# Turned probabilities copied by ScalarE alone, and a second PSUM tile for the first head's relative scores, in a relative-position cross attention

## The chip, the cores and the metric

One core of a Trainium2 chip runs the whole program. The metric is the device time of one execution in microseconds, taken as the median of the runs shown. All times below count from the start of the profiled span.

## What is computed

The program is a chain of six layers, each added to x. The change lies in the fourth, the cross attention of the second block (`cross1`):

```python
content = einsum('bthd,bThd->bhtT', q + r_w_bias, k)
rel = einsum('bthd,bThd->bhtT', q + r_r_bias, pe)   # pe: projected sinusoids
rel = _relative_shift(rel)
attn = (content + rel) * (1.0 / sqrt(HEAD_DIM))
attn = attn * mask - 10000000000.0 * (1.0 - mask)
p = softmax(attn, axis=-1)
out = einsum('bhtT,bThd->bthd', p, v).reshape(b, t, DMODEL)
```

There are 256 query tokens, 4096 keys, 16 heads of 16 columns, all in float32. The shift moves every row of the relative scores by an amount that depends on the row, across the whole matrix.

## The kernel before, in words

**Units.** The scores of one head are 256 x 4096. They are cut into four units (`U` = 4): two tiles of 128 query rows by two halves of 2048 keys. A unit has two parts of 1024 keys (`SUB`), and the layer has 64 units (`UNITS`).

**The way of a unit.** TensorE makes the relative scores of a part in the PSUM tile `rel_ps` (`relative`, L1821; four matmuls in all use two 32-row groups of the array, part 0 the first two groups and part 1 the last two). ScalarE copies them to `out0` or `out1` (`evacuate`, L1928). SP stores the unit's 1 MB to DRAM (`store`, L1774) with a row pitch one longer than the row, and reads it back shifted, a part at a time, into `row` (`read_back`, L1763). TensorE makes the content scores in `cont_ps` (`content`, L1821), VectorE adds them to `row` (`add`, L2011), GpSimd multiplies by the mask (L1989), VectorE adds the mask's complement `minus` and takes the maximum (`top_of`, L2020), ScalarE takes the exponential (L1933). Then TensorE turns a part by eight 128x128 transposes into `turn_ps` (`turn`, L1852), it is copied to `turned`, and TensorE weighs the values with it (`weigh`, L1867). The sums go through `sumsT` (VectorE, L2041) and one more matmul (`bring_together`, L1876) to `o_all` (L2046).

**Who copies what is turned.** Part 0 is copied by ScalarE whole (L1939, 1024 columns). Part 1 is copied half by ScalarE (`copy_left`, L1946, 512 columns) and half by VectorE (`copy_turned`, L2035, 512 columns).

**The order.** It is written out by hand. Every engine runs `slots`: slot n works on the relative scores of unit n+4, the content scores, sum and mask of unit n, the maximum and exponential of unit n-1, the turning and weighing of unit n-2, and the gathering of unit n-3. Slots -4 to 2 and the last ones are written out, and the others stand in a hardware loop over pairs of heads. Slots -4 to -1 therefore hold only the first head's relative scores and the second head's queries (`turn_weights` L1969, the product L1840, `make_queries` L2072). I call them the opening. In them TensorE and ScalarE take turns on the one tile `rel_ps`. VectorE makes `minus` (L2082) ahead of all slots. In TensorE's program the second part of unit n+3 comes first in slot n, ahead of the content scores of unit n.

## Time and profile before

| | |
|---|---|
| median of 3 runs | 1489.84 us (1487.76 to 1493.67) |
| profiled execution, its own time | 1488.5 us |
| its span | 1486.7 us |
| busy shares of the span | TensorE 80%, VectorE 65%, ScalarE 60%, GpSimd 26% |
| this layer | from about 736 us to 1307 us for the part with the slots |

A row of the timeline gives the start, the duration, the engine and the line; PE is TensorE's matmul, PEld its weight load, DVE is VectorE, ACT ScalarE, POOL GpSimd, SPq SP's DMA queue. The brackets hold the idle time of the engine before the instruction and what released it. `xN` means N instructions merged into a row. L1821 is one line for both kinds of scores, so the tile's name tells them apart.

### The profile page before, as it was taken

What the parts mean: (1) busy time and instruction counts of PE and PEld (TensorE: products, weight loads), DVE (VectorE), ACT (ScalarE), POOL (GpSimd) and SP (SyncE); (2) the same over time, 40 slices, a digit from 0 to 9 for tenths busy, and PEclk for the clock granted to TensorE, in tenths of its full rate; (3) what the DMA queues carried; (4) which work ended last, traced back from release to release, by engine and by line L of the source; (5) the groups of instructions that cost most, each with busy time, mean ns of one, the idle gap of its engine ahead of it and who ended that gap; (6) DMA issues with size and microseconds to landing.
All of it is one profiled execution on the core that took longest, in us unless ns stands there. A gap on an engine that the chain in (4) does not pass through costs nothing. (4 is left out here: it accounts for less than half of the span.)

```text
span 1486.7 us, 25581 instructions
## 1 busy us (share of the span) xinstructions
PE 1195.8 (80%) x8423; PEld 716.1 (48%) x8423; DVE 969.3 (65%) x1633; ACT 894.2 (60%) x1243; POOL 383.8 (26%) x149
## 2 busy tenths in 40 slices
PE   7677777739999768799768888888888888746798
PEld 3343344324444446688624544444444444424587
DVE  5798898950110566522228999999999999835321
ACT  3699999948889335233226666676766667413210
POOL 1000000000000040000006767676676766600000
PEclk9899999969999778899957999999999999877899
DMA  7864544448552420044648888888888888251050
GB/s 264 269 169 111 120 121 106 100 102 158 109 105 45 163 89 1 29 145 152 219 159 300 283 286 275 285 283 285 290 278 286 274 289 282 96 162 59 1 170 7
DMA packets 97048, 257.51 MB, mean 173 GB/s; under 512 B 11193, under 2 KB 41305, under 8 KB 85466
## 3 DMA queue, kind: packets, MB, share of 16 engines
q1 hardware_dynamic: 96992, 256.79, 55.7%
q8 instruction: 32, 0.52, 0.1%
q14 instruction: 24, 0.20, 0.0%
HBM read 165.31 MB, written 91.92 MB: 173 GB/s over the span
## 5 line engine op out<-in xcount | busy, mean ns | idle before, releaser
L1989 POOL TENSOR_TENSOR xb_row<-xb_row,w_mask 128x1024 f32<-128x1024 f32 x128 | 359.3, 2827 | 376.0 <-DVE xb_row L2011 376.0
L2020 DVE CUSTOM_DVE_ANT_0 xb_row<-xb_row,xb_minus 128x1024 f32<-128x1024 f32 x128 | 266.6, 2083 | 8.4 <-POOL xb_row L1989 8.2
L1928 ACT COPY xb_out<-xb_rel_ps 128x1024 f32<-128x1024 f32 x128 | 129.9, 1015 | 132.3 <-PE xb_rel_ps L1821 132.1
L2011 DVE TENSOR_TENSOR xb_row<-xb_cont_ps,xb_row 128x1024 f32<-128x1024 f32 x128 | 155.2, 1213 | 24.7 <-PE xb_cont_ps L1821 24.2
L1852 PEld LDWEIGHTS xb_turn_ps<-_ident,xb_row 128*128 128x128 f32 x1024 | 118.5, 149 | 103.5 <-ACT xb_row L1933 52.0
L1821 PE MATMUL xb_rel_ps<-xb_kk,xb_qq 32*128 32x512 f32 x512 | 157.3, 692 | 10.8 <-ACT xb_out L1928 9.5
L567 DVE TENSOR_REDUCE xa_stats<-xa_b_ps 128x1 f32<-128x1024 f32 x128 | 153.2, 1220 | 7.3 <-PE xa_b_ps L466 7.1
L828 ACT ACTIVATE xa_probs<-xa_psT,xa_t_now 128x1024 f32<-128x1024 f32 x128 | 141.2, 1114 | 25.3 <-PE xa_psT L787 25.2
L1821 PE MATMUL xb_cont_ps<-xb_kk,xb_qq 32*128 32x512 f32 x512 | 152.6, 673 | 2.9 <-DVE xb_row L2011 2.9
L1852 PE MATMUL xb_turn_ps<-_ident,xb_row 128*128 128x128 f32 x1024 | 151.2, 295 | 4.3 <-ACT xb_row L1933 2.3
L516 ACT ACTIVATE xa_exps<-xa_b_ps,xa_stats 128x1024 f32<-128x1024 f32 x128 | 142.7, 1115 | 3.6 <-DVE xa_stats L567 2.1
L1484 POOL TENSOR_TENSOR b_tc<-b_raw,w_waves 128x512 f32<-128x512 f32 x4 | 5.1, 1269 | 533.4 <-ACT b_raw L1470 533.4
L1933 ACT ACTIVATE xb_row<-xb_row,xb_ntop 128x2048 f32<-128x2048 f32 x64 | 128.3, 2005 | 0.0
L1867 PE MATMUL xb_sum_ps<-xb_turned,xb_vhead 128*17 128x128 f32 x2048 | 86.5, 296 | 24.8 <-DVE xb_turned L2035 24.8
L466 PE MATMUL xa_b_ps<-xa_k,xa_q 96*128 96x512 bf16 x256 | 77.5, 388 | 25.7 <-ACT xa_exps L516 13.8
L575 DVE CUSTOM_DVE_ANT_0 xa_squares<-xa_exps 128x1024 f32<-128x1024 f32 x64 | 78.4, 1225 | 25.1 <-ACT xa_exps L516 25.1
L487 PE MATMUL xa_b_ps<-xa_wv,xa_ctxT 128*128 x512 | 67.0, 285 | 17.9 <-ACT xa_exps L516 17.9
L760 PE MATMUL xa_sums<-xa_probs,xa_vhead 128*17 128x256 f32 x1024 | 80.8, 389 | 0.2 <-ACT xa_probs L828 0.2
L1655 DVE SCALAR_TENSOR_TENSOR _x<-b_out_ps,b_gates,_x 128x256 f32<-128x256 f32 x64 | 27.9, 479 | 78.6 <-PE b_out_ps L1570 78.1
L487 PEld LDWEIGHTS xa_b_ps<-xa_wv,xa_ctxT 128*128 128x128 f32 x512 | 61.3, 196 | 33.2 <-ACT xa_exps L516 29.3
L1867 PEld LDWEIGHTS xb_sum_ps<-xb_turned,xb_vhead 128*17 128x17 f32 x2048 | 48.0, 102 | 57.3 <-DVE xb_turned L2035 42.8
L1946 ACT COPY xb_turned<-xb_turn_ps 128x512 f32<-128x512 f32 x64 | 37.5, 586 | 60.2 <-PE xb_turn_ps L1852 60.0
(364 smaller groups left out, 1868.3 us busy)
## 6 DMA issues: line engine op xcount, KB each, us to landing
xb_row<-rel_scores SPq DMA_DIRECT2D x128, 512.0 KB, 5.3
rel_scores<-xb_out SPq DMA_DIRECT2D x32, 1024.5 KB, 4.9
rel_scores<-xb_out SPq DMA_DIRECT2D x32, 1024.0 KB, 4.8
b_e_w<-in_L_ffn_e_w SPq DMA_DIRECT2D x32, 513.0 KB, 3.4
w_w<-in_L_ffn_w SPq DMA_DIRECT2D x24, 512.0 KB, 6.8
xa_k<-first_parts SPq DMA_DIRECT2D x24, 384.0 KB, 5.1
value_rows<-xa_values SPq DMA_DIRECT2D x16, 544.0 KB, 6.1
xb_kk<-key_blocks SPq DMA_DIRECT2D x17, 512.0 KB, 6.3
```

The source lines that it names most:

```text
L487: mm = nc.tensor.matmul(out[:, n * P:(n + 1) * P], ctxT[:, k, at:at + P], wv[:, bass.ds(it, 1), k, :], start=(k == 0), stop=(k == KC - 1))
L516: nc.scalar.activation(exps[:, u % 4], ps[:, slot % 4], ACT.Exp, scale=-1.0, bias=stats[:, c % 2, 0, u:u + 1], accum_out=stats[:, c % 2, 1 ...
L567: nc.vector.tensor_reduce(stats[:, c % 2, 0, u:u + 1], ps[:, slot % 4], AX, ALU.min).then_inc(s["min_ready"], 1)
L828: nc.scalar.activation(probs[:, g % 4].rearrange("p c n -> p (c n)"), ps[:, g % 2], ACT.Exp, scale=t_now[:, b:b + 1]).then_inc(probs_ready, 1)
L1821: mm = nc.tensor.matmul(out[:, k * BANK:(k + 1) * BANK], qq[rows, b, kind, t * P:(t + 1) * P], kk[rows, b, half], start=True, stop=True)
L1852: mm = nc.tensor.transpose(turn_ps[:, k * P:(k + 1) * P], row[:, u, at:at + P], f.ident[:])
L1867: mm = nc.tensor.matmul(sum_ps[at:at + DV, 0:P], vhead[:, b, half * NCH // 2 + part * CPS + k, :], turned[:, part, k, :], start=(part == 0 ...
L1928: nc.scalar.copy(out[:, part * SUB:(part + 1) * SUB], rel_ps[:]).then_inc(s["rel_out"], 1)
L1933: nc.scalar.activation(row[:, u], row[:, u], ACT.Exp, bias=ntop[:, u:u + 1]).then_inc(s["exp_done"], 1)
L1989: nc.gpsimd.tensor_tensor(row[:, u, at:at + SUB], row[:, u, at:at + SUB], mask[:, t, half * HALF + at:half * HALF + at + SUB], ALU.mult).t ...
L2011: nc.vector.tensor_tensor(row[:, u, at:at + SUB], cont_ps[:], row[:, u, at:at + SUB], ALU.add).then_inc(s["cont_out"], 1)
L2020: nc.vector.tensor_tensor_reduce(out=row[:, u, at:at + SUB], in0=row[:, u, at:at + SUB], in1=minus[:, t, half * HALF + at:half * HALF + at ...
```

## The change

1. ScalarE copies both parts of what is turned, 1024 columns each. VectorE's copy and the semaphore `turned_left` are gone.
2. In slots -4 to -1 TensorE makes both parts of a unit's relative scores: part 0 in `rel_ps` as before, part 1 in `cont_ps`, which is unused until slot 0 (`first_right`). ScalarE copies part 0 (and counts two on `rel_out`), VectorE copies part 1 (`evacuate_right`, with the new semaphore `fill_out`). The store of a first-head unit waits for both, and the first content scores wait for VectorE's last copy. The second part of unit 3, which stood first in slot 0, is now in slot -1.
3. VectorE makes the two tiles of `minus` in slots -2 and -1, each behind its copy, instead of ahead of all slots. The first `top_of` waits for both.

```diff
 def store(p, c):
     sp.wait_ge(s["rel_out"], 2 * n + 3)
+    if isinstance(n, int) and n < U:
+        sp.wait_ge(s["fill_out"], n + 1)
...
 def content(p, c, part):
     pe.wait_ge(s["cont_out"], 2 * n + part + 1)
+    if part == 0 and isinstance(n, int) and n == 0:
+        pe.wait_ge(s["fill_out"], U)
...
+def first_right(c):
+    if c > 0:
+        pe.wait_ge(s["fill_out"], c)
+    scores(0, c, 1, 1, cont_ps, s["rel_mm"])
...
 # TensorE's slot
-if runs(n, U - 1):
+if runs(n, U - 1) and (n is None or n > 0):
     relative(p, c + U - 1, 1)
...
 if runs(n, U):
     relative(p, c + U, 0)
+if n is not None and n < 0:
+    first_right(c + U)
...
 # ScalarE
-nc.scalar.copy(out[:, part * SUB:(part + 1) * SUB], rel_ps[:]).then_inc(s["rel_out"], 1)
+first = isinstance(n, int) and n < U
+nc.scalar.copy(out[:, part * SUB:(part + 1) * SUB], rel_ps[:]).then_inc(s["rel_out"], 2 if first else 1)
...
-nc.scalar.copy(turned[:, 1, 0:CPS // 2].rearrange("p k n -> p (k n)"), turn_ps[:, 0:BANK]
-               ).then_inc(turned_left, 1)
+act.wait_ge(s["turned"], 2 * n + part + 1)
+act.wait_ge(s["weighed"], 2 * n + part + 1)
+nc.scalar.copy(turned[:, part].rearrange("p k n -> p (k n)"), turn_ps[:]).then_inc(turned_sb[part], 1)
...
 # VectorE
+def evacuate_right(c):
+    dve.wait_ge(s["rel_mm"], 2 * c + 2)
+    if c >= NHALF:
+        dve.wait_ge(rel_stored[c - NHALF], 16)
+    out = out1 if c % NHALF else out0[:, 1:HALF + 1]
+    nc.vector.tensor_copy(out[:, SUB:HALF], cont_ps[:]).then_inc(s["fill_out"], 1)
...
-nc.vector.tensor_copy(turned[:, 1, CPS // 2:].rearrange("p k n -> p (k n)"), turn_ps[:, BANK:]
-                      ).then_inc(turned_sb[1], 1)
...
 # VectorE's slot, and the lines ahead of the slots
+if n is not None and n < 0:
+    evacuate_right(c + U)
+if n is not None and -NT <= n < 0:
+    t = n + NT
+    nc.vector.tensor_scalar(minus[:, t], mask[:, t], 1.0, 1e10, ALU.subtract, ALU.mult
+                            ).then_inc(s["minus_set"], 1)
...
-for t in range(NT):
-    nc.vector.tensor_scalar(minus[:, t], mask[:, t], 1.0, 1e10, ALU.subtract, ALU.mult
-                            ).then_inc(s["minus_set"], 1)
-dve.wait_ge(s["minus_set"], NT)
```

TensorE's queue in the opening before (`xb_both` with `xb_wturn` is the product that makes queries):

```order
L1840 MATMUL xb_both<-xb_xnT,xb_wturn 128x256 x2
L1821 MATMUL xb_rel_ps<-xb_kk,xb_qq 128x512 x4
L1840 MATMUL xb_both<-xb_xnT,xb_wturn 128x256 x2
L1821 MATMUL xb_rel_ps<-xb_kk,xb_qq 128x512 x12
L1821 MATMUL xb_cont_ps<-xb_kk,xb_qq 128x512 x2
L1821 MATMUL xb_rel_ps<-xb_kk,xb_qq 128x512 x2
L1821 MATMUL xb_cont_ps<-xb_kk,xb_qq 128x512 x2
```

And the same place with the change:

```order
L1850 MATMUL xb_both<-xb_xnT,xb_wturn 128x256 x2
L1822 MATMUL xb_rel_ps<-xb_kk,xb_qq 128x512 x2
L1822 MATMUL xb_cont_ps<-xb_kk,xb_qq 128x512 x2
L1850 MATMUL xb_both<-xb_xnT,xb_wturn 128x256 x2
L1822 MATMUL xb_rel_ps<-xb_kk,xb_qq 128x512 x2
L1822 MATMUL xb_cont_ps<-xb_kk,xb_qq 128x512 x2
L1822 MATMUL xb_rel_ps<-xb_kk,xb_qq 128x512 x2
L1822 MATMUL xb_cont_ps<-xb_kk,xb_qq 128x512 x2
L1822 MATMUL xb_rel_ps<-xb_kk,xb_qq 128x512 x2
L1822 MATMUL xb_cont_ps<-xb_kk,xb_qq 128x512 x4
L1822 MATMUL xb_rel_ps<-xb_kk,xb_qq 128x512 x2
L1822 MATMUL xb_cont_ps<-xb_kk,xb_qq 128x512 x2
```

The query products keep their places. Every unit's two parts stand as a pair in two tiles, and the first content scores (the last two of the row with x4) follow the fourth pair directly.

VectorE's queue in the opening before:

```order
L2079 TENSOR_TENSOR xb_qbias<-xb_qbias,xb_rbias 128x17
L2072 TENSOR_SCALAR xb_qq<-xb_both,xb_qbias,xb_kinds 128x256 x2
L2082 TENSOR_SCALAR xb_minus<-w_mask 128x4096 x2
L2072 TENSOR_SCALAR xb_qq<-xb_both,xb_qbias,xb_kinds 128x256 x2
L2011 TENSOR_TENSOR xb_row<-xb_cont_ps,xb_row 128x1024 x2
```

And with the change:

```order
L2087 TENSOR_TENSOR xb_qbias<-xb_qbias,xb_rbias 128x17
L2080 TENSOR_SCALAR xb_qq<-xb_both,xb_qbias,xb_kinds 128x256 x2
L2012 COPY xb_out<-xb_cont_ps 128x1024 x2
L2080 TENSOR_SCALAR xb_qq<-xb_both,xb_qbias,xb_kinds 128x256 x2
L2012 COPY xb_out<-xb_cont_ps 128x1024
L2058 TENSOR_SCALAR xb_minus<-w_mask 128x4096
L2012 COPY xb_out<-xb_cont_ps 128x1024
L2058 TENSOR_SCALAR xb_minus<-w_mask 128x4096
L2020 TENSOR_TENSOR xb_row<-xb_cont_ps,xb_row 128x1024 x2
```

Four copies are new, and the two tiles of `minus` stand behind the third and the fourth.

## Rows read from the trace of the kernel before

**Rows 1.** Windows view, steady part. Engines' busy us (instructions), TensorE clock, DMA share, GB/s
```profile
1000.00:1050.00 50.00, 41.94 (x424) 24.22 (x428) 48.12 (x73) 34.60 (x33) 34.99 (x14) 0.97 0.84 286
```

**Rows 2.** Timeline, GpSimd: start us, duration us, engine, line, operation, [idle before <-releaser]
```profile
777.14 2.34 POOL L1989 TENSOR_TENSOR xb_row<-xb_row,w_mask 128x1024 f32<-128x1024 f32 x1 [217.69 <-DVE xb_row L2011]
780.62 3.26 POOL L1989 TENSOR_TENSOR xb_row<-xb_row,w_mask 128x1024 f32<-128x1024 f32 x1 [1.13 <-DVE xb_row L2011]
...
802.25 5.61 POOL L1989 TENSOR_TENSOR xb_row<-xb_row,w_mask 128x1024 f32<-128x1024 f32 x2 [2.50 <-DVE xb_row L2011]
...
1005.12 5.61 POOL L1989 TENSOR_TENSOR xb_row<-xb_row,w_mask 128x1024 f32<-128x1024 f32 x2 [2.50 <-DVE xb_row L2011]
...
1289.10 5.60 POOL L1989 TENSOR_TENSOR xb_row<-xb_row,w_mask 128x1024 f32<-128x1024 f32 x2 [2.50 <-DVE xb_row L2011]
```

**Rows 3.** Timeline, VectorE, one pass of the loop
```profile
1004.97 1.21 DVE L2020 CUSTOM_DVE_ANT_0 xb_row<-xb_row,xb_minus 128x1024 f32<-128x1024 f32 x1
...
1006.47 1.22 DVE L2011 TENSOR_TENSOR xb_row<-xb_cont_ps,xb_row 128x1024 f32<-128x1024 f32 x1
...
1007.61 0.68 DVE L2035 COPY xb_turned<-xb_turn_ps 128x512 f32<-128x512 f32 x1
...
1008.60 3.21 DVE L2020 CUSTOM_DVE_ANT_0 xb_row<-xb_row,xb_minus 128x1024 f32<-128x1024 f32 x1 [0.23 <-POOL xb_row L1989]
```

**Rows 4.** Timeline, TensorE and ScalarE, the same pass
```profile
1003.97 0.40 PE L1876 MATMUL xb_both<-xb_gather,xb_sumsT 128*128 128x17 f32 x2 [0.99 <-DVE xb_sumsT L2041]
...
1007.28 0.59 ACT L1946 COPY xb_turned<-xb_turn_ps 128x512 f32<-128x512 f32 x1 [0.80 <-PE xb_turn_ps L1852]
...
1008.34 0.63 PE L1867 MATMUL xb_sum_ps<-xb_turned,xb_vhead 128*17 128x128 f32 x16 [0.53 <-DVE xb_turned L2035]
...
1009.97 0.86 PEld L1852 LDWEIGHTS xb_turn_ps<-_ident,xb_row 128*128 128x128 f32 x8 [0.76 <-ACT xb_row L1933]
```

**Rows 5.** Timeline, the opening: first head's relative scores to the first add
```profile
748.63 4.48 DVE L2082 TENSOR_SCALAR xb_minus<-w_mask 128x4096 f32<-128x4096 f32 x2
...
751.03 1.01 ACT L1928 COPY xb_out<-xb_rel_ps 128x1024 f32<-128x1024 f32 x1 [5.56 <-PE xb_rel_ps L1821]
...
752.10 2.08 PE L1821 MATMUL xb_rel_ps<-xb_kk,xb_qq 32*128 32x512 f32 x4 [1.10 <-ACT xb_out L1928]
...
755.59 2.08 PE L1840 MATMUL xb_both<-xb_xnT,xb_wturn 128*128 128x256 f32 x4 [1.42 <-ACT xb_wturn L1969]
...
773.54 1.22 PE L1821 MATMUL xb_rel_ps<-xb_kk,xb_qq 32*128 32x512 f32 x2 [1.11 <-ACT xb_out L1928]
...
773.65 1.22 PE L1821 MATMUL xb_cont_ps<-xb_kk,xb_qq 32*128 32x512 f32 x2
...
775.84 1.23 DVE L2011 TENSOR_TENSOR xb_row<-xb_cont_ps,xb_row 128x1024 f32<-128x1024 f32 x1 [17.05 <-PE xb_cont_ps L1821]
```

**Rows 6.** DMA view, 736 to 800 us: transfers, KB each, median us to landing
```profile
xb_row<-rel_scores SPq DMA_DIRECT2D x9, 512.0 KB, 6.0
rel_scores<-xb_out SPq DMA_DIRECT2D x3, 1024.5 KB, 5.2
```

**Rows 7.** Timeline, SP's queue, the first read back
```profile
768.28 0.35 SPq L1763 DMA_DIRECT2D xb_row<-rel_scores  x1
```

**Rows 8.** Windows view, the opening's clock and DMA share (columns as in rows 1)
```profile
780.00:784.00 4.00, 3.26 (x9) 1.43 (x10) 2.89 (x4) 1.32 (x2) 3.26 (x1) 0.50 0.99 333
...
792.00:796.00 4.00, 4.00 (x17) 2.17 (x18) 3.03 (x7) 1.84 (x3) 2.37 (x1) 0.51 0.70 236
796.00:800.00 4.00, 3.56 (x52) 2.15 (x52) 3.92 (x3) 3.76 (x4) 3.27 (x2) 1.00 0.76 225
```

**Rows 9.** Timeline, the end of the loop
```profile
1299.17 0.59 ACT L1946 COPY xb_turned<-xb_turn_ps 128x512 f32<-128x512 f32 x1 [2.12 <-PE xb_turn_ps L1852]
...
1305.10 0.69 DVE L2035 COPY xb_turned<-xb_turn_ps 128x512 f32<-128x512 f32 x1 [3.77 <-PE xb_turn_ps L1852]
...
1305.85 0.63 PE L1867 MATMUL xb_sum_ps<-xb_turned,xb_vhead 128*17 128x128 f32 x16 [0.22 <-DVE xb_turned L2035]
```

More of the change, by code:

```diff
@@ L1847, in turn @@
                     pe.wait_ge(turned_sb[1 - part], n + 1)
-                    if part == 0:
-                        pe.wait_ge(turned_left, n + 1)
                     for k in range(CPS):
@@ L1858, in weigh @@
                     pe.wait_ge(turned_sb[part], n + 1 + part)
-                    if part == 1:
-                        pe.wait_ge(turned_left, n + 2)
                     if u == 0 and part == 0:
@@ L1933, in exponentials, with copy_turned @@
                     nc.scalar.activation(row[:, u], row[:, u], ACT.Exp, bias=ntop[:, u:u + 1]).then_inc(s["exp_done"], 1)
[L1935 removed]
+                def copy_turned(p, c, part):
                     n, head, u, b, t, half = where(p, c)
[L1937 to L1947 removed]
+                    act.wait_ge(s["turned"], 2 * n + part + 1)
+                    act.wait_ge(s["weighed"], 2 * n + part + 1)
+                    nc.scalar.copy(turned[:, part].rearrange("p k n -> p (k n)"), turn_ps[:]).then_inc(turned_sb[part], 1)
                 def slot(p, c, n):
                     if runs(n, -2):
[L1951 removed]
+                        copy_turned(p, c - 2, 0)
                     if runs(n, U):
@@ L1954, in slot @@
                     if runs(n, -2):
-                        copy_left(p, c - 2)
+                        copy_turned(p, c - 2, 1)
                     if runs(n, -1):
                         exponentials(p, c - 1)
-                    if runs(n, U):
+                    if runs(n, U) and (n is None or n >= 0):
                         evacuate(p, c + U, 1)
@@ L2017, in top_of @@
                     dve.wait_ge(s["masked"], 2 * n + part + 1)
+                    if part == 0 and isinstance(n, int) and n == 0:
+                        dve.wait_ge(s["minus_set"], NT)
                     dve.sem_inc(s["top_begun"], 1)
@@ L2029, in top_of @@
                                                 top2[:, u, 1:2], -1.0, ALU.max, ALU.mult).then_inc(s["top_kept"], 1)
-                def copy_turned(p, c):
-                    n, head, u, b, t, half = where(p, c)
-                    dve.wait_ge(s["turned"], 2 * n + 2)
-                    dve.wait_ge(s["weighed"], 2 * n + 2)
-                    nc.vector.tensor_copy(turned[:, 1, CPS // 2:].rearrange("p k n -> p (k n)"), turn_ps[:, BANK:]
-                                          ).then_inc(turned_sb[1], 1)
                 def sums_out(p, c):
@@ L2059, in slot @@
                         add(p, c, 1)
-                    if runs(n, -2):
-                        copy_turned(p, c - 2)
                     if runs(n, -3):
```

13 lines of the change are left out of this document (1 added, 12 removed).

## The prediction

> **What bounds the kernel now.** I read the windows view of the loop first. VectorE looks like the bound there: busy 48.12 of 50 us, ScalarE only 34.60 [rows 1]. That reading would make its copy the thing to remove. The timeline of GpSimd says otherwise. Its masks come in pairs of 5.61 us, each pair after an idle 2.50 us that VectorE's add ends [rows 2], and from 802.25 to 1289.10 us 60 slots pass in 486.85 us, 8.11 each, which is 5.61 + 2.50. The add that ends the idle time comes behind VectorE's 3.21 us maximum, and that row is stretched: the same instruction takes 1.21 at 1004.97 [rows 3]. The long one starts at 1008.60, just after the first mask of the pair that began at 1005.12, and ends at 1011.81, which is 1.08 after GpSimd's pair ends at 1010.73 [rows 2, 3]. So VectorE counts as busy while it waits for GpSimd's second mask. The loop is a ring: two masks, the last 1.08 of a maximum, a small copy, an add, and again the masks. The first mask of a pair is stretched too: 2.34 alone (777.14), 3.26 beside a maximum (780.62) [rows 2]; 5.61 is 2.34 + 3.27.
>
> The Trainium skill (SBUF — State Buffer, Who interferes with whom) says that GpSimd and VectorE share a port pair that one of them holds for a whole instruction, and that a VectorE instruction with two SBUF inputs meets a GpSimd one there. The trace agrees: 3.21 against 1.21. The same section lists copies among what can take the pair, under conditions on their operands; by that alone each of VectorE's 0.68 us copies would hold the masks up, and the change would give back some 60 x 0.68 = 41 us.
>
> Then the opening, 749 to 776 us. One tile is filled in 2.08 us and emptied in 1.01, in turn, so a part takes about 3.19 (751.03 to the end of the next matmuls at 754.18) [rows 5]. VectorE waits 17.05 us for the first content scores, and TensorE is what it waits for [rows 5].
>
> **Part 1, the copies in the loop.** Removed from VectorE: 0.68 us a slot [rows 3]. In the ring this buys nothing. VectorE's copy ends at 1008.29, and its next maximum cannot end before GpSimd's pair ends plus 1.08, whenever it starts. Without the copy VectorE waits 0.6 us longer for the same mask. I take 0; the ends are 0 and -0.68 a slot. Nor did the copy slow the masks: 3.27 in the loop with it, 3.26 at 780.62 without it [rows 2].
> Added to ScalarE: 1.01 instead of 0.59, +0.43 a slot (a 1024-column copy as at 751.03) [rows 4, 5]. ScalarE has some 15 us of 50 free [rows 1]. Three things wait behind that copy:
> - The weighing of part 1. It began at 1008.34, 0.05 after VectorE's copy. ScalarE's long copy, from 1007.28, ends at 1008.29 [rows 4]: no change.
> - The exponential, and behind it TensorE's transposes at 1009.97, which waited for it [rows 4]. They move to 1010.4 and end at about 1011.5. TensorE's next instruction waits for VectorE and comes one period after 1003.97, at 1012.08 [rows 4]. The slack was 1.0 and 0.6 is left.
> - ScalarE's next copies, in front of which it idles anyway.
> So 0 a slot. If 0.43 came through in every slot it would be +26.
>
> **Part 2, the opening.** Worked with 2.08 for the matmuls of a part, 1.01 for ScalarE's copy, 2.08 for the query product, 2.28 for one tile of `minus` (half of 4.48 and an overlap) [rows 5]. The new VectorE copy of 1024 columns from PSUM is not in the loop; the nearest rows are its add over the same PSUM columns, 1.23, and its 512-column copy, 0.68, which doubled gives 1.36 [rows 3, 5]. I take 1.22. Two parts in two tiles use different row groups. The trace shows such a pair at 773.54 and 773.65, side by side [rows 5], so a pair costs about 2.2 and not 4.2.
> - Unit 0: matmuls 748.9 to 751.1, copies out by 752.4.
> - ScalarE prepares the query weights (0.4) after one copy instead of two. The product runs 752.4 to 754.4; it was at 755.59 [rows 5].
> - Unit 1: 754.4 to 756.6, out by 757.9. Unit 2: 757.6 to 760.1, out by 761.4; then `minus` to 763.7. Unit 3: from 760.8, second part 761.5 to 763.5; VectorE is free at 763.7 and copies to 764.9; second `minus` to 767.1.
> - First content scores 764.9 to 767.0, first add at 767.3 instead of 775.84 [rows 5]: -8.5.
> - Another 0.9 follows. Before, unit 4's relative scores had to wait until unit 3's last part (773.54) was made and copied, to 776.7. Now they follow the content scores at 767.0, 9.7 earlier. Through ScalarE's copies they gate the next query product, hence the fourth add. From there everything runs 9.4 earlier.
> `minus` costs nothing: VectorE had 17 us to wait. It delays the last copy by 0.2.
> Do the transfers follow? The first read back was issued at 768.28 [rows 7], as the store of unit 1 landed. That store can now go at 758.0, and with 4.2 to 5.2 for landing [rows 6] the read back goes at 762.2 to 763.2, 5 to 6 us earlier. A read back takes 6.0 in the median [rows 6], so it lands by 768.2, near the 767.3 wanted. Between there and 784 the DMA engines were nearly full before (0.99) [rows 8], and VectorE never waited for them. I put them just outside the path.
> Sum for the opening: -9.4, with -5.5 as the small end (all shifts as the first read back does) and -12 as the large (TensorE at full clock one slot sooner).
>
> **Part 3, the end.** After the last masks nothing hides ScalarE's copy. Behind it stand two exponentials (the last starts after the copy at 1299.17) and the last weighing, which waited for VectorE's 0.69 us copy (1305.10, then 1305.85) [rows 9]. 0.43 + 0.43 + 0.32 = +1.2.
>
> **Sum.** -9.4 + 0 + 1.2 = -8.2. Against the profiled execution's 1488.5 us that gives 1480.3. The median of the runs is 1.3 higher and would give 1481.6. I say **1481**.
>
> **The rivals.**
> - **The transfers hold the opening.** For: the full DMA engines, and a read back that starts only 5 to 6 us earlier. Against: VectorE waited for TensorE, not for them. Opening -5.5, end +1.2: **1484.5**.
> - **The pairs do not overlap**, or the two copies hold each other up. A unit then takes some 5.3 instead of 6.4, four units give 4.4 in place of 8.5: also about 1485. Against: the pair at 773.54.
> - **The clock.** TensorE's granted clock was 0.50 from the opening until about 796 us, and rose after a stretch in which TensorE was busy without a gap (4.00 of 4.00) [rows 8]. If a denser opening lifts it one slot sooner, or the end runs at the full clock, 3 us more go: **1478**. The other way costs as much. The Trainium skill (TensorE: Matmul & The Clock Gate, Part 1) says that activity releases the half clock and that the same kernel shows different numbers of slow matmuls from run to run; by that this case is open in either direction.
> - **VectorE is the bound after all**, and the copy's 0.68 comes back 60 times: **1440**. Against: the 3.21 us rows.
> - **Slower: ScalarE's longer copy joins the ring.** It delays the exponential, the transposes behind it, and with them the content scores that VectorE adds. It decides once the transposes come over 1.0 us late; I count 0.43. In a slot with a query product, ScalarE's weight copy adds 0.4 to that, which leaves little, and at half clock the transposes take 1.0 longer. If 0.43 came through everywhere: 1480.3 + 26 = **1506**; in one slot in four, 1487.
>
> **How the numbers follow.** A measurement of this kernel tells about 0.5%, 7.4 us, from no change, so faster means below 1482.4. Forecast 0.60, its own range 1478.5 to 1483.5, of which 0.46 lies below 1482.4. Transfers 0.20, no overlap 0.03, both within 0.5%. Clock 0.07 and VectorE 0.04, both faster. ScalarE 0.06: slower 0.04, the mild form within 0.5% 0.02. Together faster 0.57, same 0.39, slower 0.04. The range of 1476 to 1487 takes in the forecast, the transfers, the clock and the mild form. The first read backs and the clock are its width.
>
> **What would show it.** Right: GpSimd's first mask near 768.5 instead of 777.14; the eight first-head copies in four pairs about 3.4 us apart; mask pairs still every 8.11 us, and VectorE idle for some 0.8 us ahead of the long maximum where it was 0.23; the loop reaching its pace near 793; the last mask pair near 1279.7; the stretch from there to the layer's last sums about 1.2 longer. Wrong: a period other than 8.11 (VectorE or ScalarE was in the ring), an add of the first three units released by a DMA, or pairs of matmuls in the opening that take over 4 us.

## The result, and the profile after

| | before | changed |
|---|---|---|
| median, 9 executions each on one chip | 1493.6 us (1487.76 to 1500.84) | 1485.21 us (1480.63 to 1491.19) |
| profiled execution, own time | 1488.5 us | 1491.19 us |
| its span | 1486.7 us | 1489.4 us |
| VectorE busy | 969.3 us | 941.3 us |
| ScalarE busy | 894.2 us | 913.0 us |
| GpSimd busy | 383.8 us | 386.6 us |

The ratio is 0.9954, with a 95% interval of 0.9935 to 0.9972: 6.8 us less, give or take 2.7 (the two medians differ by 8.4). The predicted 1481 was worked against a median of 1489.84 of three runs; on nine runs the same kernel came out at 1493.6, and 8.2 less than that is 1485.4.

The profiled execution of the change is the slowest of its nine, and its span is 2.7 us longer than the one before. So the two traces are not read by their spans but by landmarks inside the layer. All landmarks below count from the layer's first VectorE instruction (it clears the tile of the weighted sums, `xb_sum_ps`), which no part of the change touches: it started at 736.43 us before and at 741.52 in the changed trace, and those 5.1 us belong to earlier layers.

| from the layer's start, us | before | changed | moved by |
|---|---|---|---|
| GpSimd's first mask | 40.71 | 31.98 | -8.7 |
| unit 3's first mask | 65.82 | 54.96 | -10.9 |
| one slot, unit 3 to unit 60 | 8.11 | 8.11 | 0.0 |
| unit 60's first mask | 528.34 | 517.29 | -11.1 |
| last sums of the layer | 570.90 | 566.11 | -4.8 |
| from there to the end of the span | 179.35 | 181.78 | +2.4 |

The opening gave 10.9 us, the loop nothing, and the stretch from unit 60 to the layer's last sums took 6.3 back. Four views show how. The 2.4 us more behind the layer lie in a part of the program that the change doesn't touch; the account of the sum comes back to them.

**The loop.** Windows view of the changed kernel, columns as in [rows 1]:

```profile
1000.00:1050.00 50.00, 42.65 (x418) 24.26 (x418) 46.28 (x69) 36.29 (x33) 34.97 (x13) 0.97 0.86 290
```

VectorE is 1.84 us less busy in 50, ScalarE 1.69 more, and GpSimd stands at 34.97 as before. The timeline of one pass, changed kernel, to be held against [rows 2 to 4]:

```profile
999.26 5.61 POOL L1990 TENSOR_TENSOR xb_row<-xb_row,w_mask 128x1024 f32<-128x1024 f32 x2 [2.51 <-DVE xb_row L2020]
...
1001.42 1.01 ACT L1948 COPY xb_turned<-xb_turn_ps 128x1024 f32<-128x1024 f32 x1 [0.81 <-PE xb_turn_ps L1860]
...
1002.49 0.63 PE L1873 MATMUL xb_sum_ps<-xb_turned,xb_vhead 128*17 128x128 f32 x16 [0.54 <-ACT xb_turned L1948]
1002.73 3.22 DVE L2031 CUSTOM_DVE_ANT_0 xb_row<-xb_row,xb_minus 128x1024 f32<-128x1024 f32 x1 [0.82 <-POOL xb_row L1990]
```

The pair of masks is 5.61 again and the idle time ahead of it 2.51. The maximum still takes 3.22. VectorE waits 0.82 ahead of it where it waited 0.23: the time of the removed copy has become a wait for the same mask.

**The opening.** Timeline of the changed kernel, to be held against [rows 5] and [rows 7]:

```profile
756.28 1.23 DVE L2012 COPY xb_out<-xb_cont_ps 128x1024 f32<-128x1024 f32 x1 [2.38 <-PE xb_cont_ps L1822]
...
761.83 1.22 DVE L2012 COPY xb_out<-xb_cont_ps 128x1024 f32<-128x1024 f32 x1 [4.32 <-PE xb_cont_ps L1822]
...
765.23 1.23 DVE L2012 COPY xb_out<-xb_cont_ps 128x1024 f32<-128x1024 f32 x1 [1.27 <-PE xb_cont_ps L1822]
...
766.37 2.28 DVE L2058 TENSOR_SCALAR xb_minus<-w_mask 128x4096 f32<-128x4096 f32 x1
...
767.08 0.34 SPq L1762 DMA_DIRECT2D xb_row<-rel_scores  x1
...
768.29 1.01 ACT L1937 COPY xb_out<-xb_rel_ps 128x1024 f32<-128x1024 f32 x1 [2.22 <-PE xb_rel_ps L1822]
768.64 1.22 DVE L2012 COPY xb_out<-xb_cont_ps 128x1024 f32<-128x1024 f32 x1
...
770.01 2.08 PE L1822 MATMUL xb_cont_ps<-xb_kk,xb_qq 32*128 32x512 f32 x4 [1.42 <-DVE xb_out L2012]
...
773.50 2.34 POOL L1990 TENSOR_TENSOR xb_row<-xb_row,w_mask 128x1024 f32<-128x1024 f32 x1 [209.33 <-DVE xb_row L2020]
```

VectorE's copies start at 756.28, 761.83 (a query product lies between), 765.23 and 768.64, so the pairs stand 3.4 apart once they follow each other. The last VectorE copy starts 0.35 after ScalarE's (768.29), behind `minus`. The first read back is issued 25.56 us after the layer's start, 31.85 before.

**Slot 2**, where the opening gave more than foretold. Timeline, changed kernel:

```profile
792.63 1.23 DVE L2031 CUSTOM_DVE_ANT_0 xb_row<-xb_row,xb_minus 128x1024 f32<-128x1024 f32 x1
...
792.73 3.35 POOL L1990 TENSOR_TENSOR xb_row<-xb_row,w_mask 128x1024 f32<-128x1024 f32 x1 [0.28 <-DVE xb_row L2020]
...
796.48 5.61 POOL L1990 TENSOR_TENSOR xb_row<-xb_row,w_mask 128x1024 f32<-128x1024 f32 x2 [0.40 <-DVE xb_row L2020]
```

And the same place in the trace before:

```profile
797.22 0.68 DVE L2035 COPY xb_turned<-xb_turn_ps 128x512 f32<-128x512 f32 x1
797.38 2.37 POOL L1989 TENSOR_TENSOR xb_row<-xb_row,w_mask 128x1024 f32<-128x1024 f32 x1 [0.47 <-DVE xb_row L2011]
797.81 3.01 DVE L2020 CUSTOM_DVE_ANT_0 xb_row<-xb_row,xb_minus 128x1024 f32<-128x1024 f32 x1
```

Before, the mask started at 797.38 while VectorE copied, so the maximum came second and took 3.01. Now there is no copy, the maximum starts 0.10 ahead of the mask and takes 1.23, and the mask is the stretched one (3.35 against 2.37). The next mask waits 0.40, where it waited 2.50 before [rows 2].

**The end.** Windows view from 1268 us, changed kernel:

```profile
1268.00:1274.00 6.00, 5.88 (x50) 3.06 (x49) 5.17 (x8) 2.92 (x2) 4.50 (x2) 0.57 0.33 107
1274.00:1280.00 6.00, 6.00 (x36) 3.93 (x34) 4.79 (x9) 1.60 (x2) 4.36 (x2) 0.50 0.00 1
1280.00:1286.00 6.00, 5.89 (x40) 3.50 (x34) 2.67 (x6) 2.85 (x3) 3.29 (x2) 0.50 0.01 3
1286.00:1292.00 6.00, 5.63 (x44) 2.69 (x42) 3.00 (x9) 2.87 (x3) 5.12 (x2) 0.50 0.00 0
```

The same view before:

```profile
1274.00:1280.00 6.00, 5.82 (x56) 3.83 (x54) 5.45 (x9) 2.80 (x3) 4.49 (x2) 0.73 0.32 88
1280.00:1286.00 6.00, 4.74 (x52) 2.46 (x53) 5.73 (x9) 3.19 (x3) 5.01 (x2) 1.00 0.01 3
1286.00:1292.00 6.00, 4.24 (x34) 2.70 (x37) 5.96 (x10) 1.52 (x3) 3.50 (x2) 0.90 0.00 0
```

TensorE's granted clock goes to half here in both. In the trace before it comes back after 3.4 us; in the changed one it stays down for 30.7. TensorE is then busy nearly without a gap and becomes the bound. GpSimd's timeline in the changed kernel:

```profile
1278.90 3.36 POOL L1990 TENSOR_TENSOR xb_row<-xb_row,w_mask 128x1024 f32<-128x1024 f32 x1 [0.64 <-DVE xb_row L2020]
...
1289.12 3.35 POOL L1990 TENSOR_TENSOR xb_row<-xb_row,w_mask 128x1024 f32<-128x1024 f32 x1 [0.89 <-DVE xb_row L2020]
```

These are the second masks of the last two slots with masks, 10.22 us apart instead of 8.11. From unit 60's first mask to the end of the last one it is 33.66 us here (1292.47 is its end) and 29.93 before (1294.70 [rows 2]): 3.7 of the 6.3 us. The other 2.5 come behind the last mask. Whether the long half-clock stretch belongs to the change is what several experiments ask.

### The profile page after: what moved, and what is told of

Its sections match the earlier page's. It is cut to its first block and busy times, and to the rows that moved or that the text cites. A ratio compares the mean times of both kernels' runs of the same rounds, so it can differ in the third digit from the quotient of the medians.

```text
span 1489.4 us, 25395 instructions
## 1 busy us (share of the span) xinstructions
PE 1209.5 (81%) x8423; PEld 723.6 (49%) x8423; DVE 941.3 (63%) x1573; ACT 913.0 (61%) x1239; POOL 386.6 (26%) x149
## 5 line engine op out<-in xcount | busy, mean ns | idle before, releaser
L2031 DVE CUSTOM_DVE_ANT_0 xb_row<-xb_row,xb_minus 128x1024 f32<-128x1024 f32 x128 | 273.8, 2139 | 37.1 <-POOL xb_row L1990 37.1
L1937 ACT COPY xb_out<-xb_rel_ps 128x1024 f32<-128x1024 f32 x124 | 125.3, 1011 | 98.5 <-PE xb_rel_ps L1822 83.5
L1948 ACT COPY xb_turned<-xb_turn_ps 128x1024 f32<-128x1024 f32 x128 | 129.6, 1012 | 79.4 <-PE xb_turn_ps L1860 78.8
L1860 PE MATMUL xb_turn_ps<-_ident,xb_row 128*128 128x128 f32 x1024 | 154.6, 299 | 14.0 <-ACT xb_row L1942 11.4
L1822 PE MATMUL xb_cont_ps<-xb_kk,xb_qq 32*128 32x512 f32 x528 | 162.2, 693 | 2.9 <-DVE xb_row L2020 1.5
L1822 PE MATMUL xb_rel_ps<-xb_kk,xb_qq 32*128 32x512 f32 x496 | 148.2, 675 | 4.5 <-ACT xb_out L1937 3.2
L1873 PE MATMUL xb_sum_ps<-xb_turned,xb_vhead 128*17 128x128 f32 x2048 | 92.5, 305 | 27.8 <-ACT xb_turned L1948 25.9
L487 PEld LDWEIGHTS xa_b_ps<-xa_wv,xa_ctxT 128*128 128x128 f32 x512 | 61.3, 195 | 34.1 <-ACT xa_exps L516 32.3
```

The source lines that it names most:

```text
L487: mm = nc.tensor.matmul(out[:, n * P:(n + 1) * P], ctxT[:, k, at:at + P], wv[:, bass.ds(it, 1), k, :], start=(k == 0), stop=(k == KC - 1))
L1822: mm = nc.tensor.matmul(out[:, k * BANK:(k + 1) * BANK], qq[rows, b, kind, t * P:(t + 1) * P], kk[rows, b, half], start=True, stop=True)
L1860: mm = nc.tensor.transpose(turn_ps[:, k * P:(k + 1) * P], row[:, u, at:at + P], f.ident[:])
L1873: mm = nc.tensor.matmul(sum_ps[at:at + DV, 0:P], vhead[:, b, half * NCH // 2 + part * CPS + k, :], turned[:, part, k, :], start=(part == 0 ...
L1948: nc.scalar.copy(turned[:, part].rearrange("p k n -> p (k n)"), turn_ps[:]).then_inc(turned_sb[part], 1)
L2031: nc.vector.tensor_tensor_reduce(out=row[:, u, at:at + SUB], in0=row[:, u, at:at + SUB], in1=minus[:, t, half * HALF + at:half * HALF + at ...
```

## The experiments

Two theories stood at the start. One is the prediction's: the loop is GpSimd's ring, which the copies don't touch, and the whole gain is the opening's. Its rival on the end says that ScalarE's whole copies keep TensorE at half clock there and cost some 6 us every time. All traces are read by the same landmarks; the table holds them for every run, and each experiment points into it. "Half clock" is the time at 1.2 GHz between unit 60's first mask and the last sums, and "slot" is the mean from unit 3 to unit 60.

| kernel | first mask | unit 3's mask | slot | unit 60's mask to last sums | half clock in it | layer to last sums | copies at the end |
|---|---|---|---|---|---|---|---|
| before | 40.71 | 65.82 | 8.11 | 42.56 | 13.7 | 570.90 | split |
| b0 | 40.12 | 65.24 | 8.11 | 43.50 | 13.7 | 571.06 | split |
| e2 | 40.27 | 64.51 | 8.13 | 44.94 | 17.1 | 572.67 | whole |
| changed | 31.98 | 54.96 | 8.11 | 48.82 | 34.1 | 566.11 | whole |
| e0 | 31.78 | 54.89 | 8.11 | 48.79 | 34.1 | 566.05 | whole |
| e7 | 32.87 | 56.93 | 8.11 | 43.61 | 10.2 | 562.77 | whole |
| e1 | 32.23 | 56.19 | 8.11 | 41.12 | 6.8 | 559.72 | split |
| e5 | 31.44 | 54.63 | 8.11 | 41.97 | 6.8 | 558.98 | split |
| e8 | 32.24 | 56.19 | 8.11 | 44.09 | 13.7 | 562.79 | whole |
| e3 | 30.43 | 54.36 | 8.11 | 42.58 | 10.2 | 559.36 | whole |
| e6 | 30.52 | 54.46 | 8.11 | 42.60 | 10.2 | 559.44 | whole |
| e4 | 33.46 | 58.11 | 8.13 | 50.92 | 44.4 | 572.71 | whole |
| m1 | 30.63 | 54.40 | 7.47 | 41.88 | 6.8 | 521.92 | whole |
| m2 | 30.51 | 53.04 | 7.35 | 41.20 | 6.8 | 513.31 | split |

A mean can hide single slots. The 8.13 of e2 is 8.11 but for one slot of 8.96, and that of e4 is 8.11 but for two, of 8.96 and 8.61. Both slots of 8.96 begin as TensorE's clock goes to half for 6.8 us. No trace with split copies has such a stretch in its loop, so whether the whole copy has a share in these slots isn't shown.

**e0, the changed kernel again**, with no edit.

> The changed kernel once more, for its spread and a second trace. Theory A (the opening gives all, the loop nothing, the end costs the longer copy and otherwise depends on TensorE's granted clock there): 7 to 9 us below the kernel before; in the trace the first mask is some 8.7 us and the fourth unit's mask some 10.9 us earlier than before, counted from the layer's first instruction, mask pairs stand 8.11 us apart, and the stretch from the mask pair of unit 61 to the last gathered sums lies anywhere between 35.5 us (clock mostly full) and 41 us (clock at half), against 34.45 in the one trace of before. Theory B (the longer copies of ScalarE let TensorE idle and so hold its clock down at the end every time): that stretch is 40 us or more again.

Measured: 1484.89 us, median of nine, ratio 0.9952 (0.9926 to 0.9979). Its landmarks agree with the first trace within 0.2 us, the end among them (48.79). Two traces with the same long end spoke for the rival.

**e1, the opening alone.** Part 1 of the change is undone: ScalarE copies half of part 1 and VectorE the other half.

```diff
 # ScalarE, from the changed kernel
-nc.scalar.copy(turned[:, part].rearrange("p k n -> p (k n)"), turn_ps[:]).then_inc(turned_sb[part], 1)
+nc.scalar.copy(turned[:, 1, 0:CPS // 2].rearrange("p k n -> p (k n)"), turn_ps[:, 0:BANK]
+               ).then_inc(turned_left, 1)
...
 # VectorE's slot
+if runs(n, -2):
+    copy_turned(p, c - 2)
...
```

> The changed kernel with the split copies of the kernel before put back (ScalarE 1024 + 512 columns, VectorE 512); only the opening is changed. Theory A: 1.2 us faster than the changed kernel, 8 to 10 us below the kernel before, mask pairs 8.11 us apart. Theory B: the end takes 34 to 35 us as in the kernel before, so 11 us below the kernel before and 4 to 6 below the changed kernel. Rival C (VectorE's removed copy gave part of the gain after all): slower than the changed kernel.

Measured: 1482.83 us, median of twelve, ratio 0.9938 (0.9916 to 0.9960). The opening alone is worth at least what the whole change is. The period is 8.11 with VectorE's copy as without it. Unit 3's mask comes 1.2 later than in the changed kernel, and VectorE's timeline of slot 2 says why:

```profile
790.41 0.68 DVE L2060 COPY xb_turned<-xb_turn_ps 128x512 f32<-128x512 f32 x1
791.01 3.01 DVE L2045 CUSTOM_DVE_ANT_0 xb_row<-xb_row,xb_minus 128x1024 f32<-128x1024 f32 x1
```

With the copy back, the maximum comes behind GpSimd's mask again and takes 3.01, as before.

**e2, the copies alone.** The kernel before, with ScalarE's whole copies and nothing of the opening.

```diff
 # from the kernel before
-nc.scalar.copy(turned[:, 1, 0:CPS // 2].rearrange("p k n -> p (k n)"), turn_ps[:, 0:BANK]
-               ).then_inc(turned_left, 1)
+nc.scalar.copy(turned[:, part].rearrange("p k n -> p (k n)"), turn_ps[:]).then_inc(turned_sb[part], 1)
...
 # VectorE's slot
-if runs(n, -2):
-    copy_turned(p, c - 2)
...
```

> The kernel before with ScalarE copying both parts of what is turned and nothing else. Theory A: +1.2 us against the kernel before, mask pairs 8.11 us apart, VectorE idle 0.8 us ahead of its long maximum. Theory B: +5 to +7 us, all at the end, with the clock at half there. Rival C: faster than the kernel before.

Measured: 1495.51 us, median of twelve, ratio 1.0023 (0.9998 to 1.0047). By the table it gains 1.3 at unit 3 (0.7 against b0), where in slot 2 the maximum again gets ahead of the mask, and loses 1.4 to 2.4 at the end. One slot of the loop took 8.96 instead of 8.11. The copies alone bring no gain, and probably a small loss.

**b0, the kernel before again**, to see how much of the end varies by itself.

> The kernel before once more, for a second trace of its end. Theory A: the stretch from the mask pair of unit 61 to the last gathered sums differs from 34.45 us by what the granted clock is there. Theory B: 34 to 35 us again.

Measured: 1492.14 us. The end is 43.50 at the same 13.7 us of half clock (42.56 in the first trace), so the end of one kernel moves by 0.9 us with nothing changed.

**e3, the complement ahead of the slots.** The two tiles of `minus` go back to where they stood; the rest is the changed kernel.

```diff
 # VectorE's slot, from the changed kernel
-if n is not None and -NT <= n < 0:
-    t = n + NT
-    nc.vector.tensor_scalar(minus[:, t], mask[:, t], 1.0, 1e10, ALU.subtract, ALU.mult
-                            ).then_inc(s["minus_set"], 1)
 # ahead of the slots
+for t in range(NT):
+    nc.vector.tensor_scalar(minus[:, t], mask[:, t], 1.0, 1e10, ALU.subtract, ALU.mult
+                            ).then_inc(s["minus_set"], 1)
+dve.wait_ge(s["minus_set"], NT)
```

> The changed kernel with the two tiles of the mask's complement made ahead of all slots again. VectorE is then busy 4.48 us when the first right half is ready: its first copy starts some 2 us later than in the changed kernel (56.3 to 58.3 counted so). If the complement's new place mattered, the first mask comes 2 us or more later than the changed kernel's 31.8 to 32.0 us after the layer's first instruction. Theory A: it does not matter, because the second unit waits for the query product anyway: first mask within 0.5 us of the changed kernel's. The mask pairs stay 8.11 us apart.

Measured: 1484.6 us in one execution; the first mask comes 1.6 us earlier than in the first trace of the changed kernel, and unit 3's 0.6. Timeline of e3:

```profile
754.09 4.49 DVE L2086 TENSOR_SCALAR xb_minus<-w_mask 128x4096 f32<-128x4096 f32 x2
758.61 1.23 DVE L2012 COPY xb_out<-xb_cont_ps 128x1024 f32<-128x1024 f32 x1
...
759.92 1.22 PE L1822 MATMUL xb_rel_ps<-xb_kk,xb_qq 32*128 32x512 f32 x2
...
762.88 0.70 PE L1822 MATMUL xb_rel_ps<-xb_kk,xb_qq 32*128 32x512 f32 x2 [1.17 <-ACT xb_out L1937]
...
767.70 1.22 DVE L2012 COPY xb_out<-xb_cont_ps 128x1024 f32<-128x1024 f32 x1 [2.18 <-PE xb_cont_ps L1822]
...
771.34 1.23 DVE L2020 TENSOR_TENSOR xb_row<-xb_cont_ps,xb_row 128x1024 f32<-128x1024 f32 x1 [2.41 <-DMA xb_row<-rel_scores]
```

`minus` holds the first VectorE copy up until 758.61, some 2 us after its scores are made. That costs nothing: the second unit's matmuls start at 759.92 behind the query product either way. I had expected the first mask within 0.5 us of the changed kernel's, or 2 us later, and it came earlier than both. Two things differ. Nothing stands in front of the last copy any more. And TensorE runs at full clock for a few us around 762 (0.70 us for two matmuls instead of 1.22), which the changed kernel does not show in any of its three traces. Now the first add waits 2.41 us for the read back: the transfers, which the prediction put just outside the path, are on it once the rest is that much faster.

The trace of m1, further down, parts the two. Its opening is the changed kernel's, with `minus` in the slots, but its clock rose as e3's did:

```profile
761.50 0.70 PE L1822 MATMUL xb_rel_ps<-xb_kk,xb_qq 32*128 32x512 f32 x2 [1.17 <-ACT xb_out L1937]
...
770.13 1.22 DVE L2021 TENSOR_TENSOR xb_row<-xb_cont_ps,xb_row 128x1024 f32<-128x1024 f32 x1 [0.41 <-DMA xb_row<-rel_scores]
```

Its first mask comes at 30.63, against 30.43 and 30.52 with `minus` ahead of the slots (e3, e6). So nearly all of the earlier start goes with the clock, and the place of `minus` is worth 0.1 to 0.2 us.

**e4, two tiles but one engine.** ScalarE makes both copies in the opening; the second tile stays.

```diff
 # VectorE, from the changed kernel
-nc.vector.tensor_copy(out[:, SUB:HALF], cont_ps[:]).then_inc(s["fill_out"], 1)
 # ScalarE, right behind its copy of the left half
+nc.scalar.copy(out[:, SUB:HALF], cont_ps[:]).then_inc(s["fill_out"], 1)
```

> The changed kernel with both PSUM tiles in the opening, but ScalarE making all eight copies. It separates the second tile from the second engine. Worked from the changed kernel's trace: a unit then takes 2.1 (matmuls) and 2 x 1.01 (copies) where it took about 3.4, and the query weights come 1.0 later: first mask 3 to 4 us later than the changed kernel's 31.9, so near 35.5, against 40.1 to 40.7 before. If the tile alone gave the gain: 32 to 33. If the engine alone gave it: 40.

Measured: 1495.7 us in one execution, with the longest half-clock end of all (44.4 us, end 50.92). In the opening the first mask comes at 33.46, 7.3 us earlier than before with the second engine taken away. Rows of the timeline of e4 show why so much stays:

```profile
761.16 1.01 ACT L1937 COPY xb_out<-xb_rel_ps 128x1024 f32<-128x1024 f32 x1 [4.24 <-PE xb_cont_ps L1822]
762.07 1.02 ACT L1942 COPY xb_out<-xb_cont_ps 128x1024 f32<-128x1024 f32 x1
763.45 1.01 ACT L1937 COPY xb_out<-xb_rel_ps 128x1024 f32<-128x1024 f32 x1 [0.36 <-issue]
...
771.42 1.22 DVE L2019 TENSOR_TENSOR xb_row<-xb_cont_ps,xb_row 128x1024 f32<-128x1024 f32 x1 [6.94 <-DMA xb_row<-rel_scores]
```

TensorE fills one tile while ScalarE empties the other, so the copies run nearly back to back, where before each waited for its matmuls [rows 5]. Two tiles are the larger part of the gain, the second engine the smaller. How small depends on the clock: TensorE's rose for a while in e4's opening too. Against the first trace of the changed kernel, without such a rise, the second engine is worth 1.5 us; against e3, e6 and m1, with one, 2.8 to 3.0, near the 3 to 4 that I had worked out. The first add of e4 waits for its read back, so what the single engine delays is the store.

**e5, whole copies in the loop, split ones in the last six units.** If the whole copies matter only where no mask hides them, this is the better of both.

```diff
 # ScalarE, from the changed kernel (SPLIT = UNITS - 6)
+if part == 1 and split(n):
+    nc.scalar.copy(turned[:, 1, 0:CPS // 2].rearrange("p k n -> p (k n)"), turn_ps[:, 0:BANK]
+                   ).then_inc(turned_left, 1)
+    return
...
 # VectorE's slot
+if runs(n, -2) and n is not None and split(n - 2):
+    copy_turned(p, c - 2)
...
```

> The changed kernel, but for the last six units the turned part 1 is copied half by ScalarE and half by VectorE as before. Theory A with the clock left to chance: 1.2 us below the changed kernel, the stretch from the masks of unit 60 to the last gathered sums anywhere from 41 to 48 us. Theory B (long copies at the end keep TensorE at half clock): that stretch 41 to 42 us, 5 to 7 below the changed kernel's 48.8, and the time that of the opening alone, ratio 0.993 to the kernel before.

Measured: 1482.93 us, median of twelve, ratio 0.9939 (0.9919 to 0.9959). It keeps the early slot 2 (unit 3's mask at 54.63) and has a short end (41.97), and its layer is the shortest of those in which GpSimd masks alone: 558.98.

**m1, GpSimd's mask shared.** The direct test of the ring: the last 512 of part 1's 1024 columns are masked by VectorE right behind its second add, and GpSimd masks the others.

```diff
 # GpSimd, from the changed kernel
-nc.gpsimd.tensor_tensor(row[:, u, at:at + SUB], row[:, u, at:at + SUB],
-                        mask[:, t, half * HALF + at:half * HALF + at + SUB],
+w = SUB - 512 if part == 1 else SUB
+nc.gpsimd.tensor_tensor(row[:, u, at:at + w], row[:, u, at:at + w],
+                        mask[:, t, half * HALF + at:half * HALF + at + w],
                         ALU.mult).then_inc(s["masked"], 1)
 # VectorE, behind the second add
+at = HALF - 512
+nc.vector.tensor_tensor(row[:, u, at:HALF], row[:, u, at:HALF],
+                        mask[:, t, half * HALF + at:half * HALF + HALF], ALU.mult
+                        ).then_inc(s["masked_too"], 1)
...
```

> The changed kernel, with the last 512 columns of every unit's second part masked by VectorE instead of GpSimd, right behind VectorE's second add, in the time that the removed copy freed. If GpSimd's masks set the period (theory A): GpSimd's second mask falls from 2.34 to about 1.2, VectorE's own 512 columns add some 0.7 under the shared port, and the period falls from 8.11 to about 7.7, 24 us over 60 slots. If VectorE's work or ScalarE's set the period (rival C): the period grows by 0.7 or stays at 8.11.

Measured: ratio 0.9681 (0.9648 to 0.9713); five executions took 1443.34 to 1451.71 us, and one 2146.68, which the ratio leaves out. VectorE has more to do than before and the slot is shorter, 7.47. Timeline of m1 in the loop:

```profile
1004.27 4.97 POOL L1991 TENSOR_TENSOR xb_row<-xb_row,w_mask 128x1024 f32<-128x1024 f32 x2 [2.50 <-DVE xb_row L2021]
...
1006.87 1.23 DVE L2028 TENSOR_TENSOR xb_row<-xb_row,w_mask 128x512 f32<-128x512 f32 x1
...
1008.11 2.21 DVE L2042 CUSTOM_DVE_ANT_0 xb_row<-xb_row,xb_minus 128x1024 f32<-128x1024 f32 x1
```

(The row of GpSimd merges two masks and shows the width of the first.) The first mask takes some 3.27, until 1007.54. VectorE's own mask, begun at 1006.87, has to wait for it and ends at 1008.10. Then GpSimd's 512 columns follow and end at 1009.24. The pair takes 4.97 instead of 5.61 and the idle 2.50 stays, so the slot is 7.47. I had put it at 7.7, with the pair too long by 0.2. Rival C, by which the slot would not shorten, falls.

**e6, e3 timed.** The same kernel as e3, in nine executions.

> The changed kernel with the complement ahead of all slots once more, now timed, because its first look had the first mask 1.4 us earlier than the changed kernel (30.4 against 31.9) and TensorE at half clock 7 us less in the opening. If the complement's new place in the queue costs that: the same again, first mask 30.4 to 30.8, and 1 to 2 us below the changed kernel's 1485. If the clock alone did it: first mask 31.5 to 32. The end, with ScalarE's whole copies, is one more sample: 48.8 (three of six traces with whole copies had TensorE at half clock through it) or 42 to 45.

Measured: 1483.27 us, ratio 0.9945 (0.9923 to 0.9968). The landmarks repeat e3's within 0.1 us, and the stretch of full clock in the opening is there again (37.5 us of half clock up to unit 3, 41.0 in e3, 47.8 in each trace of the changed kernel). Against the changed kernel's ratios the intervals overlap widely: the earlier masks are seen in the traces, and not in the times. One thing differs from e3. In slot 2 VectorE's maximum comes behind the mask here, though there is no copy ahead of it:

```profile
790.22 3.34 DVE L2031 CUSTOM_DVE_ANT_0 xb_row<-xb_row,xb_minus 128x1024 f32<-128x1024 f32 x1 [0.18 <-POOL xb_row L1990]
```

So removing the copy makes the early maximum likely there, not certain.

**e7, the changed kernel a third time**, for its end.

> The changed kernel a third time, for its end. If whole copies bring the long half clock every time in this kernel: 48.8 us from the masks of unit 60 to the last sums. If it is left to where the clock's drop falls: 42 to 49. First mask 31.4 to 32.

Measured: 1482.71 us in one execution, and an end of 43.61 with 10.2 us of half clock. Windows view of e7:

```profile
1268.00:1274.00 6.00, 4.33 (x37) 2.56 (x37) 5.96 (x9) 1.83 (x3) 3.50 (x2) 1.00 0.09 35
1274.00:1280.00 6.00, 3.79 (x48) 2.14 (x38) 5.18 (x7) 3.79 (x3) 3.50 (x3) 1.00 0.01 3
1280.00:1286.00 6.00, 4.63 (x45) 2.60 (x44) 5.15 (x7) 2.92 (x2) 5.38 (x2) 0.72 0.00 0
```

The same kernel, the same place, at full clock. The rival that says "every time" falls with this run.

**e8, split copies in the loop, whole ones in the last six units**: the mirror of e5.

```diff
 # ScalarE, from e1 (WHOLE = UNITS - 6)
+if whole(n):
+    nc.scalar.copy(turned[:, 1].rearrange("p k n -> p (k n)"), turn_ps[:]).then_inc(turned_sb[1], 1)
+    return
 # VectorE's slot
-if runs(n, -2):
+if runs(n, -2) and not (n is not None and whole(n - 2)):
     copy_turned(p, c - 2)
```

> The opening of the change with the split copies in the loop, but in the last six units ScalarE copies both parts whole: the counterpart of the kernel split at the end. If whole copies at the end cost the clock (theory B in the weaker form, sometimes): median 1.5 to 4 us above the opening alone (1482.8), so 1484.5 to 1487, and the end 44 to 49 us. Theory A: 1.2 us above it, the end 42.5 to 44 when the clock is mostly full.

Measured: 1484.63 us, median of twelve, ratio 0.9967 (0.9941 to 0.9992). Up to unit 60 it is e1 (32.24, 56.19, 8.11), and its end is 44.09 against e1's 41.12, with twice the half clock. Both theories had a place for such an end and such a median (44 to 49 and 1484.5 to 1487 the one, 42.5 to 44 the other), so e8 doesn't decide between them.

**m2, the mask shared further, with e3's and e5's edits.** VectorE masks 768 of part 1's columns, `minus` stands ahead of the slots, and the last six units are split.

```diff
-w = SUB - 512 if part == 1 else SUB
+w = SUB - 768 if part == 1 else SUB
...
-at = HALF - 512
+at = HALF - 768
```

> What the runs so far point to, in one kernel: the two-tile opening, the complement ahead of the slots, split copies in the last six units, and 768 columns of every second part masked by VectorE instead of 512. With 512 the masks' 4.97 us and the fixed 2.50 gave 7.47. With 768 the second mask of GpSimd is about 0.6 us, and waits 0.8 for VectorE's: 3.27 + 0.8 + 0.6 + 2.50 = 7.2 a slot, 16 us less than with 512 columns, so 1431 us. If the transfers (DMA share 0.86 at 8.11) or TensorE come in between, the period stays at 7.3 to 7.5.

Measured: ratio 0.9663 (0.9628 to 0.9698); five executions took 1433.02 to 1446.25 us, and one 1949.02. Timeline of m2:

```profile
1002.18 4.68 POOL L2002 TENSOR_TENSOR xb_row<-xb_row,w_mask 128x1024 f32<-128x1024 f32 x2 [2.50 <-DVE xb_row L2032]
...
1004.78 1.50 DVE L2039 TENSOR_TENSOR xb_row<-xb_row,w_mask 128x768 f32<-128x768 f32 x1
...
1006.29 1.66 DVE L2053 CUSTOM_DVE_ANT_0 xb_row<-xb_row,xb_minus 128x1024 f32<-128x1024 f32 x1
```

The pair is down to 4.68 and 4.68 + 2.50 is 7.18; the masks at 1002.18 and 1009.37 are 7.19 apart. In such a slot the first 512 columns moved gave 0.64 us and the next 256 gave 0.28, nearly in proportion. But from unit 7 on only three slots in four are like that. The fourth, in which VectorE also makes queries, takes 7.64:

```profile
991.46 0.98 DVE L2108 TENSOR_SCALAR xb_qq<-xb_both,xb_qbias,xb_kinds 128x256 f32<-128x256 f32 x2
...
995.00 4.68 POOL L2002 TENSOR_TENSOR xb_row<-xb_row,w_mask 128x1024 f32<-128x1024 f32 x2 [2.96 <-DVE xb_row L2032]
```

GpSimd's pair is as short as in the others, and GpSimd waits 2.96 instead of 2.50 for VectorE's add. There VectorE's own work has become the bound. With three slots of over 8 us near the start of the loop, the mean from unit 3 to unit 60 is 7.35. That is why the ratio is hardly below m1's, and the five executions took 1441.50 in the median where I had expected 1431.

m1 and m2 each had one execution of six that took 1949 and 2147 us, and no other kernel of this study had one. Both let VectorE and GpSimd mask the same tile at the same time. The record has TensorE's mean granted clock for the two, 1.000 in m1's and 0.687 in m2's, where the others show 0.91 to 0.93, but no trace of either, so the cause is open. Their ratios show what the ring is made of; as kernels to use they are unfinished until that is explained.

## Why the prediction was right, and where a term was off

**The loop: right, and shown.** The period is 8.11 in every trace with GpSimd's masks untouched, whoever copies, but for one slot of e2 and two of e4. Taking work off GpSimd, and giving it to the engine that looked like the bound, took 0.64 us from each slot in m1, and 0.92 from three slots in four in m2. That is the ring of two masks plus 2.50; in the fourth slot of m2 VectorE is the bound. The delay that the prediction put at 0.43 us ahead of TensorE's second transposes came out at 0.28: they start 4.85 us after the pair of masks before and 5.13 in the changed kernel (1004.39 against 999.26), inside the 1.0 of slack. The Trainium skill (SBUF — State Buffer, Who interferes with whom) counts copies among the instructions that can take the shared port pair, but only when their operands meet conditions. The prediction's 41 us left these conditions out. No run shows them one by one; what the traces show is that VectorE's copy from PSUM does not take the pair: the masks take 5.61 with the copy and 5.61 without it.

**The opening: right in mechanism, 1.4 us short in the first trace.** First mask -8.7 against the forecast -8.5. Unit 3's mask moved by -10.9 against -9.4. The difference comes in slot 2, a term the prediction did not have: without VectorE's copy its maximum gets to the port before GpSimd's mask. The opening alone (e1) moves unit 3's mask by -9.6, the copies alone (e2) by -1.3, and together that is the 10.9. It is a small term and not a steady one. In e6 the mask was first without the copy, and in e7 the maximum was first but TensorE's clock came up later, and unit 3's mask moved by only -8.9. The three traces of the change give -10.9, -10.9 and -8.9, so -9.4 lies within their scatter. Part 1 gives about 1 us once, before the ring closes, where I had put 0.

**`minus`: right.** In the changed kernel the last VectorE copy starts 0.35 behind ScalarE's, in e3, with nothing in front of it, 0.16 (767.54 and 767.70): the delay is 0.2, as forecast. The place ahead of the slots is at least as good. e3 and e6 start the masks 1.3 to 2.4 us earlier than the three traces of the change, but m1, with `minus` in the slots and the same rise of TensorE's clock, starts them within 0.2 of e3 and e6. By these traces the difference is the clock's.

**The transfers: right.** The first read back is issued 6.3 us earlier, a little more than the "5 to 6", and no add of the first three units waits for one in any of the three traces of the change. Little was to spare: in the first trace it landed 0.8 us ahead of the first add, and in e3, e6, m1 and m2, where TensorE's clock rose in the opening, the first add waits for it.

**The end: the term that was mis-sized.** "0.43 + 0.43 + 0.32 = +1.2" measured +6.3 and +6.2 in two traces and +1.1 in the third (e7, against the first trace of before). The term counted the longer copies at full clock. What it left out is the clock of the end, which the prediction had as a rival of 3 us and "the other way costs as much"; it took 5 more in two traces of three. The table shows how the end goes by it. Whole copies: 42.6 and 43.6 us at 10.2 of half clock, 44.1 at 13.7, 44.9 at 17.1, 48.8 at 34.1, 50.9 at 44.4. Split copies: 41.1 and 42.0 at 6.8, 42.6 and 43.5 at 13.7. So at 13.7 the whole copies cost about 1 (one trace against two), as forecast, and each us at half clock costs about a quarter (an estimate: 8.3 more us of end for 34.2 more of half clock). A stretch of over 30 us at half clock came in three of the eight traces with whole copies and unshared masks, and in none of the four with split ones. That is too few to say that the copies cause it; that they can't cause it every time is shown by e7, e3, e6 and e8. The Trainium skill (TensorE: Matmul & The Clock Gate, Part 1) says that the number of slow matmuls differs between runs of one kernel; the traces agree, 10.2 against 34.1 us of half clock for the changed kernel.

**The sum.** Forecast -8.2, measured -6.8 with an interval that holds -8.2. Of the layer's length the three traces of the change show -4.8, -4.9 and -8.2 (against 570.9 and 571.1 before): the opening's -9 to -11, the end's +1 to +6. Behind the layer, in code that is the same, the three traces of the change take 181.8 to 181.9 us to the end of the span, with 67 us of it at half clock, and the two of before 179.35 and 180.78, with 56 and 63. These 1 to 2.6 us go against the gain, and whether the change has a part in them is open. By the prediction's own line of 0.5% a gain of 0.46% is not clearly faster, a case that it gave 0.39; that 1481 became 1485 is mostly the higher median of before. The rival of the transfers had 1484.5 (its terms give 1484.2, or 1485.5 from the median). That is close to the measured median, but its mechanism is not what happened: it wanted the opening to give 5.5.

The means say something similar of the copies. In twelve executions each, e1's mean is 1483.7 and e5's 1484.1, give or take 2.2; the changed kernel's are 1485.6 and 1486.6 in nine each, give or take 2.6 and 2.9; e8's is 1486.9, give or take 3.3. Whole copies at the end look 1 to 3 us dearer in these comparisons, none of which is certain alone, and e6, which has whole copies and e3's opening, has a mean of 1483.4, as low as e1's. The opening is the whole gain, and the copies' part is nothing or a small loss.
